# Rows for the choice of experts: transposed by DMA instead of on TensorE

## The reference

```python
x = x + xattn(layernorm(x), ctx, ctx, ...)          # 16 heads, softmax over 256 keys
xf = layernorm(x)
scores = softmax(xf @ Wg.T)                          # Wg: 8 x 256, the choice of experts
w, i = top_k(scores, 2);  w = w / w.sum(-1)
y = sum over the two chosen experts of w * (silu(h1) * h3) @ W2.T + ...   # with low-rank updates
x = x + y
```

## Time and profile before

| | us |
|---|---|
| median of 3 runs | 1275.03 |
| lowest and highest run | 1274.35 and 1280.24 |
| the profiled execution | 1273.23 |
| its span, first to last instruction | 1271.5 |
| mean granted TensorE clock, share of full speed | 0.996 |

### The profile page before, as it was taken

The page is one execution under the profiler, slowest core; times in us unless marked ns, Lnnn a source line. Parts: engine busy times, 40 slices in busy tenths (PEclk is TensorE's granted clock), DMA queues, the critical chain, the costliest instruction groups (busy, mean ns, idle before and its releaser), DMA issues.

```text
span 1271.5 us, 34614 instructions
## 1 busy us (share of the span) xinstructions
PE 1223.6 (96%) x11744; PEld 951.6 (75%) x11744; DVE 1024.8 (81%) x3006; ACT 804.5 (63%) x1698; POOL 582.0 (46%) x742
## 2 busy tenths in 40 slices
PE   8899999999999999999998889999999999999997
PEld 6666666666667666766664778888888888888886
DVE  4889999999999999999886776767777767777664
ACT  5378777787777877787667644545555555555443
POOL 6303435554445545454335664444444444444444
PEclk9999999999999999999999999999999999999999
DMA  7777657475665757565466466656675656555554
GB/s 226 139 188 177 125 144 168 125 165 122 156 140 146 151 132 167 125 158 96 116 153 137 148 148 102 93 74 104 103 101 90 104 74 109 83 67 68 67 69 58
DMA packets 179618, 156.33 MB, mean 123 GB/s; under 512 B 105930, under 2 KB 161274, under 8 KB 175354
## 3 DMA queue, kind: packets, MB, share of 16 engines
q1 hardware_dynamic: 153586, 119.29, 44.2%
q0 software_dynamic: 25872, 35.01, 16.4%
HBM read 69.01 MB, written 66.51 MB: 107 GB/s over the span
## 4 chain that ended last, share of the span: by engine, by line
PE 73%; DMA 9%; issue 7%; DVE 4%; POOL 3%; ACT 2%; SPq 1%; POOLq 0%; ACTq 0%; DVEq 0%
PE pv_bank L840 10%; PE st_bank L824 9%; PE s_bank L809 8%; PE bank L83 7%; DMA out_y<-y_out,f_token 7%; PE bank L85 7%; PE bank L84 7%; PE s_bank L83 3%; PE s_bank L84 3%; PE s_bank L85 3%; PE bank L730 3%; POOL f_hold L1562 2%; PE pv_bank L83 1%; PE pv_bank L84 1%; PE st_bank L85 1%
## 5 line engine op out<-in xcount | busy, mean ns | idle before, releaser
L1066 DVE TENSOR_REDUCE maxes<-s_bank 128x2 f32<-128x512 f32 x512 | 345.2, 683 | 56.3 <-PE s_bank L809 50.0
L921 ACT ACTIVATE expo<-st_bank 128x512 f32<-128x512 f32 x512 | 300.5, 597 | 64.2 <-PE st_bank L824 62.2
L1563 POOL DMA_INDIRECT out_y<-y_out,f_token x132 | 206.9, 1567 | 23.6 <-issue 12.9
L824 PE MATMUL st_bank<-stack 67*128 67x256 bf16 x1024 | 196.7, 273 | 3.8 <-ACT expo L921 3.4
L809 PE MATMUL s_bank<-stack 65*128 65x256 bf16 x1024 | 196.2, 272 | 4.0 <-DVE maxes L1066 2.0
L1562 POOL TENSOR_TENSOR f_hold<-ones 128x1 f32<-128x1 f32 x136 | 64.8, 477 | 267.7 <-ACT y_out L1719 260.9
L1719 ACT ACTIVATE y_out<-y_sum,gate 128x256 f32<-128x256 f32 x132 | 59.9, 500 | 153.8 <-DVE y_sum L1842 150.7
L1777 DVE SCALAR_TENSOR_TENSOR vals<-s_bank,b,vals 128x256 f32<-128x256 f32 x146 | 70.3, 483 | 98.4 <-ACT vals L1685 96.5
L83 PE MATMUL s_bank<-xt_hi,stack 128*128 128x256 bf16 x504 | 138.2, 274 | 3.1 <-DVE xt_hi L1759 3.1
L606 POOL DMA_INDIRECT expert_rows<-row,slot x128 | 130.2, 1017 | 21.3 <-issue 20.9
L840 PE MATMUL pv_bank<-expo,vals 128*32 128x256 f32 x2048 | 137.9, 387 | 1.1 <-ACT expo L921 1.1
(11 more groups left out here) (238 smaller groups left out, 3053.2 us busy)
## 6 DMA issues: line engine op xcount, KB each, us to landing
stack<-qk_scratch SPq DMA_DIRECT2D x256, 128.0 KB, 4.8
qk_scratch<-qk SPq DMA_DIRECT2D x32, 512.0 KB, 4.4
x<-in_x SPq DMA_DIRECT2D x16, 512.0 KB, 7.1
ctx_in<-in_ctx SPq DMA_DIRECT2D x16, 512.0 KB, 8.1
out_y<-x SPq DMA_DIRECT2D x32, 256.0 KB, 6.4
expo<-in_w_units SPq DMA_DIRECT2D x18, 256.0 KB
x<-in_w_units SPq DMA_DIRECT2D x18, 256.0 KB
expert_rows<-padding SPq DMA_DIRECT2D x14, 260.0 KB, 3.8
```

The costliest lines, as they stand in the source:

```text
L824: ins = pe.matmul(st_bank[s % 2][:, n, :], stack[k][0:COL_K, 1, h, c * P:(c + 1) * P], stack[k][0:COL_K, 0, h, :], start=True, stop=True)
L921: act.activation(expo[:, s % E_RING], st_bank[s % 2][:], ACT.Exp, scale=SCALE).then_inc(exp_done, 1)
L1066: dve.tensor_reduce(maxes[:, t, h0:h0 + 2], s_bank[r % 2][:], AX_X, ALU.max).then_inc(max_done, 1)
L1563: pool.indirect_dma_start(out=dram["y"], out_offset=bass.IndirectOffsetOnAxis(ap=tokens[turn_of(T)][:, a:a + 1], axis=0), in_=y_outs[turn_ ...
```

## The change

For all tiles but the last the two norm fills are dropped. In their place SP issues four transposing DMA transfers, one for each group of 128 tokens, which read GpSimd's halves (128 partitions x 512 bf16) in SBUF and write `rt`, now one tensor with the four parts (high and low, two halves of the 256 numbers) side by side. The gate fill waits for these transfers (`rt_loaded`), and stands in slot 24 instead of 22. The rank fill goes from 28 to 30 and the third fill of sums from 30 to 28; ScalarE's exponential, `pick` and `weigh` go two slots later too. On SP the four stand between the store of the keys and the store of the queries, and wait for the low halves and for the gate before. GpSimd waits, before it overwrites a buffer of halves, for the transposes out of it. ScalarE no longer waits for the norm fills before it overwrites `rn`.

```diff
@@ FILLS
-         (16, "norm", -1, 0), (17, "norm", -1, 1), (19, "queries", 2, 1), (20, "sums", 0, 1), (22, "gate", -1, 0),
-         (23, "heads", 0, 0), (25, "max", 1, 0), (26, "values", 1, 0), (27, "out", 0, 0), (28, "rank", -1, 0),
-         (29, "values", 1, 1), (30, "sums", 0, 2))
+         (16, "norm", -1, 0), (17, "norm", -1, 1), (19, "queries", 2, 1), (20, "sums", 0, 1), (23, "heads", 0, 0),
+         (24, "gate", -1, 0), (25, "max", 1, 0), (26, "values", 1, 0), (27, "out", 0, 0), (28, "sums", 0, 2),
+         (29, "values", 1, 1), (30, "rank", -1, 0))
+def is_filled(name, p):
+    return 0 <= p < NB and (name != "norm" or p == NB - 1)
...
-        rt = {h: sb(f"rt_{h}", [P, KC, TOK], BF16) for h in ("hi", "lo")}
+        rt_both = sb("rt", [P, 2 * KC, TOK], BF16)
+        rt = {h: rt_both[:, KC * n:KC * n + KC] for n, h in enumerate(("hi", "lo"))}
...
+            def turn_rows(p):
+                if p:
+                    sp.wait_ge(*ready(("gate", p - 1, 0)))
+                sp.wait_ge(row_lo_ready, p + 1)
+                for a in range(TT):
+                    sp.dma_start_transpose(rt_both[:, :, a * P:(a + 1) * P], row_halves[p % 2][:, a, :])\
+                        .then_inc(rt_loaded, 16)
...
                 elif on(q + 2):
                     unstack(q + 2, 1)
+                if 0 <= q - 1 < NB - 1:
+                    turn_rows(q - 1)
+                if q > -2 and on(q + 2):
                     unstack(q + 2, 0)
...
                 if p > 1:
                     pool.wait_ge(scattered[k], 16 * 2 * TT * (p // 2))
+                    pool.wait_ge(rt_loaded, 16 * TT * (p - 1))
...
             def gate(out, p, n):
-                for c in range(KC):
-                    pe.wait_ge(*free(("norm", p, c)))
+                if p < NB - 1:
+                    pe.wait_ge(rt_loaded, 16 * TT * (p + 1))
+                else:
+                    for c in range(KC):
+                        pe.wait_ge(*free(("norm", p, c)))
...
                 if n == "r" and half == 0 and p:
-                    for c in range(KC):
-                        act.wait_ge(*ready(("norm", p - 1, c)))
                     act.wait_ge(row_lo_ready, p)
...
-                    if u == 24 and 0 <= q - 1 < NB:
+                    if u == 26 and 0 <= q - 1 < NB:
                         gate_exp(q - 1)
...
-                    if u == 25 and 0 <= q - 1 < NB:
+                    if u == 27 and 0 <= q - 1 < NB:
                         pick(q - 1)
-                    if u == 27 and 0 <= q - 1 < NB:
+                    if u == 29 and 0 <= q - 1 < NB:
                         weigh(q - 1)
```

More of the change, by code:

```diff
@@ L94, in plan @@
                 order.append(("bias", 0, 0))
-            order += [(name, q + ahead, n) for s, name, ahead, n in FILLS if s == u and 0 <= q + ahead < NB]
+            order += [(name, q + ahead, n) for s, name, ahead, n in FILLS
+                      if s == u and is_filled(name, q + ahead)]
     uses, place = [0] * BANKS, {}
@@ L223, in program @@
         row_lo_ready = sem("row_lo_ready")
+        rt_loaded = sem("rt_loaded")
         row_loaded = sem("tile_row_loaded")
@@ L304, in fill_at @@
             name, ahead, n = fills_at[u]
-            return (name, q + ahead, n) if 0 <= q + ahead < NB else None
+            return (name, q + ahead, n) if is_filled(name, q + ahead) else None
         def row_slot(q, u):
```

## The result

The changed kernel takes 1357.74 us (median; 1352.62 to 1369.24), the kernel before 1276.1 on the same chip: a ratio of 1.0659, 95% interval 1.0627 to 1.069. The forecast was 1285 in a range of 1262 to 1312. The sign was right, the size was not: +82 us where +10 had been worked out. The profiled execution took 1357.54 us, its span is 1355.8. One execution of experiment 1, 1719.95 us at a clock of 0.695, is left out of its median.

The account below looks back on a forecast made before the run. TensorE was taken to set the pace. Thirteen steps at +0.7 us (1.6 standing less 0.9 saved), then +0.2 and +0.9, make +10.2 us: 1283.4 for the profiled execution, 1285 as median; range 1262 to 1312.

Parts of the forecast that it names:

- The clock: A sign of being wrong: TensorE's clock falling after the wait, counted at nothing because it stayed at 1.00 in these steps.
- The ring: SP's queue of transfers, run one after another: no transpose moves before 364.2 us, when the keys' store has landed.
- Issue on SP: SP issues four transposes after GpSimd's low halves: 2.5 to 5.2 us, ending between 363.0 and 365.7.
- The data and the wait: The transposes' 0.52 MB take 2.8 us, landing at 367.0; TensorE then stands 1.6 us before the gate.
- What is removed: Two norm fills in fifteen of sixteen row tiles: 0.93 us of TensorE a step, 14 us in 15 steps.
- What is moved: Gate fill from slot 22 to 24, behind the heads fill: counted 0, with 0.6 us a step both ways.
- plain pace: Rival: transposes out of SBUF move like plain rows, 1.2 us, no standing in 14 steps: 1262 us; chance 0.26.
- break-even: Rival: about 2.1 us for the four transposes (250 GB/s), 1275 us; chance 0.16, shared with No effect on the path.
- Slow issue: Rival: issuing on SP takes 2.23 us a transpose, TensorE stands 4.8 us a step: 1329 us; chance 0.10.
- No effect on the path: Rival: VectorE sets the pace and TensorE's savings vanish: 1275 us; chance 0.16, shared with break-even.
- The last step: SP issues the head's five transposes first; TensorE stands 2 us at the gate, less 1.2: +0.9 us.

Follow-up runs that it names:

- experiment 1: Changed kernel with ten extra 512-column matmuls on TensorE before the gate's wait for the transposes; 1341.71 us, ratio 1.053.
- Experiment 9: Kernel before plus the four unread transposes, with TensorE waiting for them behind the gate of slot 22, turns and choice unmoved; 1360.95 us, ratio 1.0659.
- experiment 6: Kernel before with only the choice of experts moved two slots later, norm fills kept, no transposes; 1313.70 us, ratio 1.0285.
- experiment 11: The early pairs: changed kernel, choice in old slots, rows split earlier, two 128 x 1024 transposes ahead of the keys' store; 1324.88 us, ratio 1.0382.
- experiment 12: Experiment 11 with the transposes also ahead of SP's eight restacks and the output's store; 1385.03 us, ratio 1.0841.
- 13: Experiment 11 with the eight restacks issued earlier, ahead of SP's wait for the row maxima; 1287.72 us, ratio 1.0088.
- 14: Changed kernel with the eight restacks issued ahead of SP's wait for the row maxima; 1344.79 us, ratio 1.0532.
- experiment 16: 13 in the middle steps alone: tiles 1 to 12 by transfer, others turned by TensorE, restacks early from the third step; 1273.17 us, ratio 0.9965.
- experiment 5: Changed kernel without transposes, gate on zeros, choice in its old slots; ten steps 400.20 us against 406.34 in the kernel before.
- 4: Changed kernel without transposes, gate on zeros, choice in the new slots; ten steps 407.33 us against 406.34 in the kernel before.
- 7: Kernel before with the four transposes issued as well into a tile nobody reads or waits for; 1275.47 us, ratio 1.0012.
- experiment 8: Changed kernel with one 128 x 2048 transposing transfer a step in place of four of 128 x 512; 1344.22 us, ratio 1.0549.

## Why the prediction was wrong

- **The clock, "which I count at nothing"**: this is the step that failed. The reason given was that the clock stands at 1.00 in the steps of the kernel before; but those steps have no wait of a microsecond in them, so they could not tell. It costs 2.94 of the 5.17 us a step, more than the idle time of the wait itself (2.13). Experiment 9 shows it with the wait alone, experiment 1 by filling the wait, and experiment 6 with 0.4 us of idle time in place of a wait. The sentence that named it as a way to be wrong was the right place to put a price: some 13 us at half speed cost 5.9 us of busy time (experiment 6), and such a fall in each of 13 steps would cost nearly 80.
- **The ring**: right in kind, but not what ends last. In the early pairs no transpose moved before the loads ahead of it were through, and moving those loads took the wait away (11 to 13). In the changed kernel the same move gives back only 0.5 us (14): there the issues set the end.
- **Issue on SP**: above the prediction's upper bound, 5.2 to 6.0 us for four instead of 2.5 to 5.2, and the prediction let it end before the data "in every case". The fourth issue of the step shown ended at 348.03, after a microsecond in which next to nothing moved. An issue takes 1.2 to 1.3 us, for 128 x 512 (median 1288 ns) as for 128 x 1024 (1262 and 1271 ns in the median of 12 and 13), and up to 5.2 us behind loads that still move (11).
- **The data and the wait**: mis-sized. The data alone are faster than taken, 290 GB/s (16), so an estimated 1.8 us for 0.52 MB instead of 2.8. Yet it is 7.8 us from ready rows to the gate instead of 6.8, and a wait of 2.3 us instead of 1.6.
- **What is removed**: 0.93 us by the starts, 1.08 by busy time, but 0.61 on the path (5, 13): TensorE's idle time rises from 0.63 to 1.1 us a step. "What TensorE saves is therefore saved in the end time" was two thirds right.
- **What is moved**: counted 0 with 0.6 both ways; it is +0.7 (4 against 5) and +1.0 (6), and brings down the clock by itself (6). The changed kernel has that fall too, in two of ten steps.
- **The rivals**: plain pace did not come, and with data at 290 GB/s, above its own break-even of 250, the change lost all the same. The Trainium skill's rule (Advanced Engine Details and Errata, X-Bar Transpose (TRN2)), that transposing DMAs are as fast as plain ones at 350 to 400 GB/s, isn't met here: experiment 16 reads 287 to 293 for them and 369 to 393 for the plain store right behind. Slow issue was nearer to the result (1329; its own terms add up to 1331), but the 2.23 us an issue that it takes did not come (median 1.29), and the rest was the clock. "No effect on the path" was refuted by 13.
- **The last step**: forecast +0.9 us from 2 us of standing, measured +12.4. TensorE stood 2.8 us, and its busy time grew from 34.29 to 44.88 us, at a clock of 0.68 instead of 0.96.

With the measured wait, savings and moved choice but no clock, ten steps would have been 22 us longer (10 x (0.10 + 2.13)); at that rate 15 steps give 33, 1309 us, just inside the range. In the ten steps the clock adds 29. Of the other 30 us, 12.4 lie in the last step; how the rest splits wasn't worked out.

## What to carry to other kernels

On an engine that is 98% busy at full clock a wait has two prices, its length and the stretch at half clock behind it; write the second into the sum when an edit puts a wait into every step. Idle time by itself doesn't tell: experiments 4, 5, 7 and 13 idle about 1 us a step at a clock of 1.00, experiment 6 loses its clock with 1.2. So read the granted clock in short stretches. Before a DMA takes over work with a deadline, list what stands ahead of it in the same ring and look for what may be issued earlier: here eight loads that nobody needed yet decided between 1.7 us of waiting and none. A saving on the engine that sets the pace may reach the end time only in part (here 0.61 of 0.93 us), so measure it with the added work left out, as in experiment 5.

## What the runs showed of the hardware

- Granted clock: after a TensorE wait of 2.2 us it went from 1.00 to 0.50 within 2 us of TensorE having started again, and was back at 1.00 some 4 us later; the second fall lasted 14 us (stretches of the changed kernel). In experiment 12, with a wait of 5.85 us until 368.24, it stood at 0.50 from 366 to 372, so it fell inside the wait. In experiment 6 it fell after a loss of 0.4 us in 4 in every other step, and not after the same loss in the steps between. The Trainium skill (TensorE: Matmul & The Clock Gate, HAM oscillation — how this bites in real kernels) describes a kernel whose matmuls wait for a DMA in every tile and start cold in each. The trace agrees with that picture in kind: a wait for a DMA in nearly every step and half clock behind it. Here the matmuls fill nearly all of a step, the wait of 2.2 us is shorter than that kernel's 3 to 5, the first matmuls behind it still run at 1.00, and experiment 6 shows the fall without a DMA.
- A transposing transfer out of SBUF costs SP 1.2 us or more to issue, whether it turns 0.13 or 0.26 MB; one of 0.52 MB took 2.86 us at least and 3.89 in the median (experiment 8). With nothing ahead 0.26 MB move at some 290 GB/s and land 2.8 us after the issue began (experiment 16).
- SP's issue itself is slower behind transfers that still move: two transposes 5.71 us behind the restacks, 2.98 us ahead of them.
- Four forms of the same transfer (four, two, one; ahead of the keys' store or behind it) ended 7.7 to 7.9 us after the last rows were ready in one step each: 350.07 - 342.23, 348.95 - 341.02, 349.39 - 341.66, 343.77 - 336.03. That they agree so closely is owed to the steps chosen: over all steps but the last the four read 5.7 to 8.8 us. In the step of experiment 11 the issue begins at 334.43, the small packets of the transposes move between 339 and 341.75, and the gate starts 2.0 us after that; why the last part is so long is not shown.
